# Decay rows written once for all channels, and the state recurrence as four scans of 128 columns an octet

## What is computed

```python
x = x + mixer(layernorm(x)); x = x + xattn(ctx, ctx, layernorm(x)); x = x + ffn(layernorm(x))
# mixer, for each of 256 channels d with N = 64 states
dt = exp(log_dt); dA = exp(-exp(log_A) * dt[:, None]); dB = B_param * dt[:, None]
h = dA * h + dB * u[..., None]          # over 1024 time steps
y = einsum('dn,bdn->bd', C_param, h) + D_param * u
y = einsum('btd,ed->bte', y, W_out) + b_out; return x + y
```

## Time and profile before

| | us |
|---|---|
| median of 3 runs | 1010.57 (1008.23 to 1010.67) |
| the profiled execution: its time | 1008.29 |
| the profiled execution: span of the core | 1006.6 |
| PE busy | 887.8 (88%) |
| DVE busy | 527.2 (52%) |
| ACT busy | 502.6 (50%) |
| POOL busy | 188.1 (19%) |
| from the first `state` matmul to the issue of `vblk` | 65.7 to 118.7 |
| `vblk` lands | 146.3 |

### The profile page before, as it was taken

The page is one execution under the profiler, slowest core; times in us unless marked ns, Lnnn a source line. Parts: engine busy times, 40 slices in busy tenths (PEclk is TensorE's granted clock), DMA queues, the critical chain, the costliest instruction groups (busy, mean ns, idle before and its releaser), DMA issues.

```text
span 1006.6 us, 15130 instructions
## 1 busy us (share of the span) xinstructions
PE 887.8 (88%) x5570; PEld 702.4 (70%) x5570; DVE 527.2 (52%) x877; ACT 502.6 (50%) x776; POOL 188.1 (19%) x207
## 2 busy tenths in 40 slices
PE   2038679669999999999999999999999999999996
PEld 0038567457787778777877777778777877777884
DVE  7975326455555555455545554556454645463411
ACT  2863514136644664466356635663566356635431
POOL 0864631022002200220022002200220021003000
PEclk9569889779999999999999999999999999999998
DMA  9976672510002000100010001000100020001000
GB/s 285 250 252 198 242 286 85 209 68 1 1 22 68 0 0 21 68 0 0 21 68 0 0 21 68 0 0 21 68 0 0 21 68 0 0 21 42 1 1 23
DMA packets 14632, 62.82 MB, mean 62 GB/s; under 512 B 2739, under 2 KB 4406, under 8 KB 13782
## 3 DMA queue, kind: packets, MB, share of 16 engines
q1 hardware_dynamic: 13862, 60.19, 17.5%
q10 hardware_dynamic: 704, 2.16, 0.7%
q0 software_dynamic: 32, 0.00, 0.0%
HBM read 50.16 MB, written 23.72 MB: 73 GB/s over the span
## 4 chain that ended last, share of the span: by engine, by line
PE 72%; DVE 12%; issue 7%; ACT 4%; DMA 4%; POOL 0%; SPq 0%; DVEq 0%; ACTq 0%; POOLq 0%
PE pair L1070 45%; PE pair L1057 10%; PE pair L1018 3%; DMA vblk<-in_ctx 3%; PE pair L1029 3%; PE pair L1045 2%; PE pair L462 2%; PE pair L995 2%; PE pair L1038 1%; DVE h1lo L889 1%; PE pair L469 1%; DVE tok L395 1%; DVE tok L391 1%; PE pair L527 1%; PE pair L476 1%
## 5 line engine op out<-in xcount | busy, mean ns | idle before, releaser
L1070 PE MATMUL pair<-h1hi,h_turned 128*128 128x512 f32 x512 | 204.7, 400 | 4.1 <-DVE h1lo L889 4.1
L770 ACT ACTIVATE vbuf<-pair,scl 128x512 f32<-128x512 f32 x128 | 87.6, 684 | 237.2 <-PE pair L1070 231.4
L1070 PE MATMUL pair<-h2hi,h_turned 128*128 128x512 f32 x512 | 202.6, 396 | 0.0
L1070 PE MATMUL pair<-h1lo,h_turned 128*128 128x512 f32 x512 | 199.8, 390 | 0.0
L1070 PE MATMUL pair<-h2lo,h_turned 128*128 128x512 f32 x512 | 199.6, 390 | 0.0
L889 DVE TENSOR_TENSOR h1lo<-vbuf,h1hi 128x512 fp32r<-128x512 f32 x80 | 61.8, 780 | 118.8 <-ACT h1hi L771 118.7
L1070 PEld LDWEIGHTS pair<-h1hi,h_turned 128*128 128x128 f32 x512 | 96.1, 188 | 39.7 <-issue 10.5
L1070 PEld LDWEIGHTS pair<-h2hi,h_turned 128*128 128x128 f32 x512 | 96.1, 188 | 25.2 <-issue 5.9
L1057 PE MATMUL pair<-zThi,w_turned 128*128 128x512 f32 x256 | 105.4, 412 | 5.2 <-DVE vbuf L918 2.6
L1070 PEld LDWEIGHTS pair<-h2lo,h_turned 128*128 128x128 f32 x512 | 96.2, 188 | 19.3
L1070 PEld LDWEIGHTS pair<-h1lo,h_turned 128*128 128x128 f32 x512 | 96.2, 188 | 18.6
(11 more groups left out here) (124 smaller groups left out, 1439.2 us busy)
## 6 DMA issues: line engine op xcount, KB each, us to landing
h_turned<-d_h SPq DMA_DIRECT2D x2, 4096.0 KB, 13.4
tok<-in_xs SPq DMA_DIRECT2D x8, 512.0 KB, 6.3
EE<-alpha_rows SPq DMA_DIRECT2D x16, 256.0 KB, 11.0
xres<-in_x SPq DMA_DIRECT2D x8, 512.0 KB, 4.0
x_rows<-x1t SPq DMA_DIRECT2D x8, 512.0 KB, 2.6
xr<-x_rows SPq DMA_DIRECT2D x8, 512.0 KB, 3.5
out<-xr SPq DMA_DIRECT2D x8, 512.0 KB, 2.7
x_rows<-xres SPq DMA_DIRECT2D x7, 512.0 KB, 2.7
```

The costliest lines, as they stand in the source:

```text
L770: e.activation(vb[:, s % 2, :], h_ps[s % 4], ACT.Gelu, scale=sc)
L1070: ins = e.matmul(bank, w[:, k, m * P:(m + 1) * P], src[part][:, k, :], start=(k == 0 and part == 0), stop=(k == HC - 1 and part == 1))
```

## The change

ScalarE writes the decay rows of all 128 pairs at once, right after `a64`, into a tile `dec` of 128 x 16 columns a partition. One memset on DVE writes the zeros of chunk 0 for all of them. The fill on DVE goes, with its waits. Since a pair's 16 decays are the same for all four sequences, the columns of `hps` and `scan` are now in the order sequence, channel, chunk, and each octet has four scans of 128 columns (8 channels x 16 chunks), one for each sequence, which all read the same 128 columns of `dec`. So `state` writes, and `carried` reads, 4 runs that lie 128 columns apart instead of 16. `scan` moves to the place of `x1t`, and `dec` (8 KB a partition) takes the place of the old `scan` and `dec`.

```diff
-    scan = sb("scan", [P, 2, BLK], "d")
-    dec = sb("dec", [P, 2, BLK], "d")
+    scan = nc.alloc_sbuf_tensor_at("scan", [P, 2, BLK], F32, offset=t["x1t_at"])
+    dec = sb("dec", [P, P, CH], "d")
...
         e.activation(a64[:, :], alT, ACT.Exp, scale=-float(L)).then_inc(pk_done, 1)
+        e.wait_ge(pk_done, 7)
+        e.activation(dec[:, :, 1:CH], a64[:, :].unsqueeze(2).to_broadcast([P, P, CH - 1]), ACT.Copy).then_inc(dec_rdy, 1)
...
-        for k in range(2):
-            e.memset(dec[:, k, :].rearrange("p (b c) -> p b c", c=CH)[:, :, 0], 0.0).then_inc(dec0, 1)
+        e.memset(dec[:, :, 0], 0.0).then_inc(dec0, 1)
...
-        e.wait_ge(dec0, 2)
-        e.wait_ge(pk_done, 7)
+        e.wait_ge(dec0, 1)
+        e.wait_ge(dec_rdy, 1)
         for o in range(NOCT):
-            dv = dec[:, o % 2, :].rearrange("p (d b c) -> p d b c", d=OCT, b=BATCH)[:, :, :, 1:CH]
-            if o >= 2:
-                e.wait_ge(h_scan, o - 1)
-            e.tensor_copy(dv, a64[:, OCT * o:OCT * o + OCT].unsqueeze(2).unsqueeze(3).to_broadcast([P, OCT, BATCH, CH - 1])).then_inc(dec_rdy, 1)
-            e.wait_ge(dec_rdy, o + 1)
+            decay = dec[:, OCT * o:OCT * o + OCT, :].rearrange("p d c -> p (d c)")
             e.wait_ge(h_ps, o + 1)
             if o >= 2:
                 e.wait_ge(y_ps, o - 1)
-            e.tensor_tensor_scan(scan[:, o % 2, :], dec[:, o % 2, :], hps[o % 2], 0.0, ALU.mult, ALU.add).then_inc(h_scan, 1)
+            for b in range(BATCH):
+                seq = slice(OCT * CH * b, OCT * CH * (b + 1))
+                ins = e.tensor_tensor_scan(scan[:, o % 2, seq], decay, hps[o % 2][:, seq], 0.0, ALU.mult, ALU.add)
+            ins.then_inc(h_scan, 1)
...
-                out = hps[o % 2][rows, c * BC:(c + 1) * BC].rearrange("p (b c) -> p b c", b=BATCH)[:, :, 1:CH]
+                out = hps[o % 2][rows, :].rearrange("p (b d c) -> p d b c", b=BATCH, d=OCT)[:, c, :, 1:CH]
...
-                ins = e.matmul(yps[o % 4][rows, c * BC:(c + 1) * BC], GG[other, i, :], scan[other, o % 2, c * BC:(c + 1) * BC], start=False, stop=(c == OCT - 1))
+                ins = e.matmul(yps[o % 4][rows, c * BC:(c + 1) * BC], GG[other, i, :], scan[other, o % 2, :].rearrange("p (b d c) -> p d b c", b=BATCH, d=OCT)[:, c], start=False, stop=(c == OCT - 1))
...
-        t["x1t"] = nc.alloc_sbuf_tensor_at("x1t", [P, TPB * DM], F32, offset=t["zone_c"] + 5 * 4096)
+        t["x1t_at"] = t["zone_c"] + 5 * 4096
+        t["x1t"] = nc.alloc_sbuf_tensor_at("x1t", [P, TPB * DM], F32, offset=t["x1t_at"])
```

## The result

The changed kernel takes 1004.68 us (median of 11 runs, 1002.41 to 1007.0), the kernel before 1009.45 us in the runs beside it (11 runs, 1006.96 to 1011.9). The ratio is 0.9958, with a 95% interval of 0.9945 to 0.9971. So it is faster by 0.42%, where 1010.7 us and no difference had been forecast. The profiled span is 1002.3 us instead of 1006.6.

A forecast was written before the change was run, and what follows sets the result against it. PE was taken to pace the octet loop, with the other 860 us untouched. Scan 0 (0.1 us) and the memset (0.05) summed to +0.15 us, all else 0: 1010.7 us on the median, range 1007.5 to 1013.5.

The forecast's parts named there:

- What bounds the kernel now: Whole span: PE paces the octet loop at 2.58 us an iteration; the remaining 860 us is untouched code.
- Fills removed: DVE's sixteen copies in the octet loop, 8.5 us, lie where DVE would wait for PE: worth 0 on the path.
- Rival D: Octet loop: the removed fills do count, behind PE's "issue" pieces; -6.2 us, 1004.4 us; chance 0.06.
- Four scans: DVE, each octet: 422 ns a scan, 1.45 us for four instead of 1.22; covered by PE in iterations 2 to 14.
- rival A: DVE's scans: a large fixed part makes four take 3.04 us, beyond PE's 2.58; +7.5 us, 1018 us; chance 0.05.
- The two places with less cover: First and last scan of the octet loop: scan 0 costs 0 to 0.2 us, taken as 0.1; scan 15 costs 0.
- (b): Scan 15, end of the octet loop: `carried` and SP's wait may come 0.23 us later, but covered: cost 0.
- ScalarE's write: All decay rows, after `a64`: 1.2 to 2.1 us inside ACT's 12.71 us wait for PE; cost 0.
- Columns: PE's `state` and `carried` in PSUM: runs 128 columns apart cost 0; bounds up to 3.8 or 32 us.
- Rival B: PE's matmuls: the new runs cost +3.8 us (1014.5 us, chance 0.03) or +13.8 us (1024.5 us, chance 0.02).
- POOL: Octet loop: POOL may gain at most 2.3 us from fills no longer conflicting, but PE never waits for it; cost 0.
- Rival C: PE's instruction waits move: 1007.6 us if faster (chance 0.04), 1013.6 us if slower (chance 0.03).

The follow-up runs named there:

- b_dve1: The kernel before with one instruction more on DVE ahead of its loop (278 instead of 277): 1006.65 us in a single run, 99.62 us an iteration.
- a_dve227: The changed kernel with 227 instructions more on DVE ahead of its loop (533 in all): 1009.68 us in one run, 100.28 us an iteration.
- a_bias_late: The changed kernel with POOL's bias adds of the loop moved behind its key products: 1002.87 us, ratio 0.9925.
- b1_bias_late: The kernel before with one instruction more on DVE and POOL's bias adds moved behind its key products: 1002.98 us, ratio 0.9941.
- b_dve64: The kernel before with 64 instructions more on DVE ahead of its loop (341): 1004.96 us in a single run, 99.64 us an iteration.

## Why the prediction was wrong

*What bounds the kernel now.* Right for the octet loop. The step that failed is the sentence "The rest of the span, 860 us, is untouched code". The lines there were untouched, but DVE's loop body had moved by 29 instructions, and each iteration changed by 0.62 us. This sentence put the effect on 85% of the span at nothing without a row for it. What the runs showed in its place: the loop gives 7 iterations and 4.67 us, and b_dve29, the kernel before with 29 idle instructions on DVE, has the whole of it.

*Fills removed.* Right: worth 0 on the path. Rival D, that they would count, is not what happened: b_dve29 keeps all fills and has the gain. That D's 1004.4 us lies so near the measured 1004.68 is chance.

*Four scans.* Right in kind: 395 ns each instead of 422, 1.35 us together instead of 1.45, since at the 267 ns taken for 128 columns the fixed part is 395 - 267 = 128 ns and not 155. The lower decomposition (two slots a column) holds; 3.04 us and rival A are excluded. In iterations 2 to 14 the slack was there, 1.24 us of idle DVE behind them.

*The two places with less cover.* Scan 15 is on the chain now, as (b) allowed. `lnv` is 0.9 us later in the profile, but the weight loads, which do not wait for scan 15, are 0.88 us later already, so nothing of it is seen to come from the scan. The 0.88 us come with "issue" pieces that differ from run to run (1.46 instead of 1.05 us at 78.5, 3.88 instead of 3.61 at 99.9), and what of them is the change's cannot be split off. It is also near the 1 us that was named as a sign of being wrong.

*ScalarE's write.* Right: 1.80 us between my bounds of 1.2 and 2.1, inside 12.7 us of wait. *Memset*: 0.17 us; with it the token passes end 0.02 us later than in the earlier trace rows, within the +0.05.

*Columns.* Right: `state` 279 ns and `within` 295, 4.65 and 4.61 ns a column, so runs 128 columns apart in PSUM cost no more than runs 16 apart did: `state` and the unbroken `within` both rose by 3 ns. Rival B is excluded. The Trainium skill, page "SBUF — State Buffer", in its note on cachelines, says that any non-contiguous access to PSUM significantly slows matmuls; this pattern does not bear it out. `carried` has a mean of 238 ns instead of 229, but its median is 219 instead of 218, and PE's pace stays at 2.59 us an iteration.

*POOL.* The conflict was weighed in too small a part of the kernel. I had weighed the conflict of DVE and POOL for the fills only, and at nothing; the conflict that decided lies in the loop over the blocks, where the change puts no instruction.

*Rival C.* Near the cause, but on the wrong engine. I took a shift in instruction waits as a matter of PE alone, "all PE instructions stay", and gave it 7%. The same question for DVE, whose stream grows by 48 scans and loses 16 fills and their waits, was not asked. The size then follows from a loop: 0.62 us is too small to see once, and seven times it is 0.4%.

*The numbers.* The sum of +0.15 us is about right for what it covers (+0.47 us up to the first store, within the scatter). The range of 1007.5 to 1013.5 was made of the scatter of the runs and the near ends of C, and left out a shift of the loop. The list of what it leaves out was short too: rival B's lower price gives 1014.5 us and C's slower case 1013.6, both above 1013.5.

What stays open: how a boundary of an instruction block delays line 918 by 0.1 us in the iterations that fetch nothing, and whether the bad place recurs every 128 or every 256 instructions. Shown are the place as the cause (b_dve29, b_dve1, a_dve227), the late start and the race. That the place is one at a block boundary rests on the packets of the first iteration and of the last block.

## What to carry to other kernels

When an edit changes the number of instructions of an engine ahead of a hardware loop, the time of the loop is not given, even if no line in it changes: compare its iteration in both profiles before crediting the edit, and run the old kernel with idle instructions of the same number. Where two engines compete for a port in a loop, look for a race decided by 0.1 us and move the competing work away from the critical one: moving POOL's bias adds brings 2.4 us on the changed kernel and leaves the bad place a cost of 0.08 us an iteration instead of 0.62. The version with both, a_bias_late, has 1002.87 us (0.9925 of before), and b1_bias_late has the same within noise with one idle instruction in place of the change. a_bias_late's lead over the changed kernel, 0.9958, is shown by the loop's 99.31 against 99.65 us an iteration, not by the intervals of the ratios, which overlap.

## What the runs showed of the hardware

- One instruction more ahead of DVE's loop changed an iteration from 100.27 to 99.62 us; 16, 29, 32 and 64 more did the same; 256 more (in the changed kernel, 227 added) gave 100.28 us again. 128 more was not run.
- DVE's instruction packets hold 8192 bytes, 128 instructions. One starts within 0.8 us after line 918's start in the first iteration of the four kernels in which that start is 0.48 us late, and none is seen from 310 to 910 us in any kernel.
- Of DVE's subtraction with two SBUF inputs and POOL's additions, the earlier one holds back the other: 1.22 us instead of 0.68 for a subtraction that starts 0.07 us late, 1.24 instead of 0.74 for an addition that starts 0.03 us late. All together take 2.36 and 3.27 us against 1.83 and 3.77 us.
- A scan over 128 columns takes 395 ns and one over 512 takes 1220, so (1220 - 395) / 384 = 2.15 ns a column and 120 ns fixed.
- An idle wait on DVE (two to an instruction) takes some 98 ns an instruction. In b_dve64 the 64 start from 119.24 to 125.41 us, the first of them beside the last scan. The profile shows 5.16 us of idle time there, counted from the scan's end, and 21.78 us in a_dve227.
